# First convolution of a four-layer network: where degrees, residual input, batch scale and activation are computed

## The reference

```python
emb = jnp.einsum('bnc,ec->bne', x_flat, dist_w)                 # 16 numbers per position
d2 = sq[:, :, None] + sq[:, None, :] - 2.0 * jnp.einsum('bne,bme->bnm', emb, emb)
...
adj = knn_mask & (dist <= THRESHOLD)                            # 24 nearest, within 10
adj = adj | jnp.eye(N, dtype=bool)[None]
X_lin = x_flat @ fc_w.T + fc_b
Dv = jnp.clip(jnp.sum(adj_f, axis=2), EPS, None)
De = jnp.clip(jnp.sum(adj_f, axis=1), EPS, None)
S = (adj_f / De[:, None, :]) @ adj_f.transpose(0, 2, 1) / Dv[:, :, None]
out_flat = S @ X_lin + x_flat
...
o = (out - mean) * rsqrt(var + BN_EPS) * bn_gamma + bn_beta     # over the batch, per channel
return o * jax.nn.sigmoid(o)
```

## Time and profile before

| | us |
|---|---|
| median of three runs | 802.1 |
| lowest, highest run | 801.76, 804.69 |
| the profiled execution, its own time | 801.38 |
| its span, first to last instruction | 799.6 |
| PE busy, share of the span | 598.2, 75% |
| DVE | 515.9, 65% |
| ACT | 378.7, 47% |
| POOL | 281.8, 35% |

### The profile page before, as it was taken

The page is one execution under the profiler, slowest core; times in us unless marked ns, Lnnn a source line. Parts: engine busy times, 40 slices in busy tenths (PEclk is TensorE's granted clock), DMA queues, the critical chain, the costliest instruction groups (busy, mean ns, idle before and its releaser), DMA issues. The chain is left out here.

```text
span 799.6 us, 8259 instructions
## 1 busy us (share of the span) xinstructions
PE 598.2 (75%) x2455; PEld 355.4 (44%) x2455; DVE 515.9 (65%) x1237; ACT 378.7 (47%) x565; POOL 281.8 (35%) x211
## 2 busy tenths in 40 slices
PE   4652779999993798482997764799596986988760
PEld 2442557777772583261444431534344334821110
DVE  2794576767764625566935564864296954759966
ACT  2102657887782450253436550472131343769930
POOL 4997167787784100301006650500101760000000
PEclk9999999999996799675996556598587995589985
DMA  3431000000001400402000000200101000000000
GB/s 105 125 98 44 0 2 1 1 1 1 0 2 36 75 0 1 148 1 79 4 1 0 1 1 10 71 1 0 63 0 27 1 1 8 1 0 0 0 0 14
DMA packets 18436, 18.44 MB, mean 23 GB/s; under 512 B 10938, under 2 KB 14331, under 8 KB 18008
## 3 DMA queue, kind: packets, MB, share of 16 engines
q1 hardware_dynamic: 18392, 17.93, 8.6%
HBM read 17.02 MB, written 0.26 MB: 22 GB/s over the span
## 5 line engine op out<-in xcount | busy, mean ns | idle before, releaser
L647 POOL TENSOR_TENSOR l0f_hid_lo<-l0f_hid,l0f_hid_hi 114x512 fp32r<-114x512 f32 (+1 forms) x75 | 97.9, 1314 | 53.3 <-ACT l0f_hid_hi L729 52.4
L825 DVE TENSOR_TENSOR l0f_hid<-l0f_silu,PS 114x512 f32<-114x512 f32 x96 | 65.6, 686 | 41.0 <-ACT l0f_silu L746 39.9
L683 PE MATMUL PS<-l0f_xs,l0w_hi 128*114 128x512 f32 x192 | 78.4, 408 | 0.0
L683 PE MATMUL PS<-l0f_xs,l0w_lo 128*114 128x512 f32 x192 | 77.2, 402 | 0.0
L746 ACT ACTIVATE l0f_silu<-PS 114x512 f32<-114x512 f32 x96 | 57.6, 600 | 31.1 <-PE PS L683 30.3
L2471 PE MATMUL PS<-l3f_ring,l3f_slots 128*32 128x512 f32 x128 | 55.7, 661 | 12.8 <-DVE l3f_ring L2548 12.8
L1303 POOL TENSOR_TENSOR l2c_den<-l2c_far,l2c_den 128x1024 f32<-128x1024 f32 x16 | 37.5, 2356 | 64.8 <-ACT l2c_den L1461 64.8
L729 ACT CAST l0f_hid_hi<-l0f_hid 114x512 fp32r<-114x512 f32 x96 | 59.1, 615 | 2.4 <-DVE l0f_hid L825 1.9
L2548 DVE SCALAR_TENSOR_TENSOR l3f_ring<-l3f_ring,l_countT 128x1024 f32<-128x1024 f32 x32 | 38.9, 1220 | 10.0 <-ACT l3f_ring L2498 10.0
L2494 ACT ACTIVATE l3f_ring<-l3r_plain,l3r_neg 128x1024 f32<-128x1024 f32 x32 | 36.0, 1134 | 14.2 <-PE PS L2471 9.7
L2542 DVE SCALAR_TENSOR_TENSOR l3f_ring<-l3f_slope,l3r_low,l3f_ring 128x1024 f32<-128x1024 f32 x32 | 40.8, 1279 | 0.9 <-ACT l3f_ring L2494 0.9
(11 more groups left out here) (571 smaller groups left out, 1359.6 us busy)
## 6 DMA issues: line engine op xcount, KB each, us to landing
l0w_raw<-in_l_w SPq DMA_DIRECT2D x32, 170.5 KB, 3.2
l3k_edge<-in_edges SPq DMA_DIRECT2D x2, 1024.0 KB
l2c_wqkv<-in_l_wqkv SPq DMA_DIRECT2D x3, 384.0 KB, 4.1
l0w_w<-in_l_w SPq DMA_DIRECT2D x8, 142.5 KB
l2f_raw<-in_l_w SPq DMA_DIRECT2D x2, 512.0 KB, 6.1
l1c_pos_w<-in_l_pos_w SPq DMA_DIRECT2D x1, 784.0 KB, 4.8
l1c_vrow<-l1c_vimg SPq DMA_DIRECT2D x7, 88.0 KB, 3.7
l1f_raw<-in_l_w SPq DMA_DIRECT2D x2, 256.0 KB
```

What stands on the lines that cost most here:

```text
L647: g.tensor_tensor(hid_lo[0:k, q % HIDS, :], hid[0:k, q % HIDS, :], hid_hi[0:k, q % HIDS, :], ALU.subtract).then_inc(S("low_pool"), 1)
L683: last = t.matmul(m.PS[0:k, (one, two)[z], :], half[:, e, z, a:a + k], xs[:, h * HALF:(h + 1) * HALF], start=(half is ew.hi), stop=(half i ...
L825: v.tensor_tensor(hid[0:k, at % HIDS, :], silu[0:k, at % RING0, :], m.PS[0:k, two, :], ALU.mult).then_inc(S("free"), 1)
```

## The change

It does six things in `l0_conv_stage`.

1. The embedding is released by halves: the semaphore `emb` counts each half, and it lies in banks 0 and 1 instead of 2 and 3. PE starts the first two images' distances when the first half's four rows are there.
2. The eight matmuls of the linear layer move behind the distances of the second image.
3. `degrees` is gone; `token_means` takes the degree from column 65 of the token product, and `edge_means(1)` moves ahead of `token_means(0)`.
4. The addition of `Xn` on DVE is gone. In place of each transpose of `mixed` PE does two plain matmuls with the identity as the moving operand, one on `Xn` and one on `mixed`, that add up in PSUM.
5. Scale and shift are made by ACT, with three dependent activations on 64 numbers, after DVE's reciprocal; a small silu ahead of them brings its table in.
6. One silu of the scaled and shifted input, by halves, writes `Y`; `lo`, `sig` and their product are gone.

```diff
         @block.scalar
...
-            a.wait_ge(S("emb"), 1)
             for h in range(2):
                 half = slice(h * HALF, (h + 1) * HALF)
+                a.wait_ge(S("emb"), h + 1)
                 if h == 0:
                     a.wait_ge(S("minus"), 4)
-                a.copy(right[0:EMB, half], m.PS[0:EMB, 2 + h, :]).then_inc(S("rows"), 1)
+                a.copy(right[0:EMB, half], m.PS[0:EMB, h, :]).then_inc(S("rows"), 1)
...
             batch_stats_scalar(a, m, C, agg, "l0c_bn")
-            a.wait_ge(m.sem("l0c_bn_affine"), 1)
+            a.activation(agg[:, 7:8], m.ident[0:C, 0:1], ACT.Silu).then_inc(S("table"), 1)
+            a.wait_ge(S("rdev"), 1)
+            a.activation(aff[:, 0:1], bn[:, 0:1], ACT.Copy, scale=agg[:, 4:5]).then_inc(S("scale"), 1)
+            a.wait_ge(S("scale"), 1)
+            a.activation(agg[:, 5:6], agg[:, 0:1], ACT.Copy, scale=aff[:, 0:1]).then_inc(S("scale"), 1)
+            a.wait_ge(S("scale"), 2)
+            a.activation(aff[:, 1:2], agg[:, 5:6], ACT.Identity, bias=bn[:, 1:2], scale=-1.0).then_inc(S("scale"), 1)
+            a.wait_ge(S("scale"), 3)
             for h in range(2):
                 part = slice(h * HALF, (h + 1) * HALF)
-                a.activation(lo[:, part], m.PS[0:C, h, :], ACT.Identity, bias=aff[:, 1:2], scale=aff[:, 0:1]).then_inc(S("act"), 1)
-                a.activation(sig[:, part], m.PS[0:C, h, :], ACT.Sigmoid, bias=aff[:, 1:2], scale=aff[:, 0:1]).then_inc(S("act"), 1)
+                a.activation(m.Y[:, part], m.PS[0:C, h, :], ACT.Silu, bias=aff[:, 1:2], scale=aff[:, 0:1]).then_inc(S("act") if h == 0 else m.sem("y_ready"), 1)
 
         @block.tensor
...
             for h in range(2):
-                last = t.matmul(m.PS[0:EMB, 2 + h, :], dist_w[:], m.XT[0:C, h * HALF:(h + 1) * HALF], start=True, stop=True)
-            last.then_inc(S("emb"), 1)
-            for j in range(NB):
-                last = t.matmul(m.PS[:, 6, j * C:(j + 1) * C], m.XT[:, j * P:(j + 1) * P], fc_w[:], start=True, stop=True)
-            last.then_inc(S("lin"), 1)
-            t.wait_ge(S("rows"), 8)
+                t.matmul(m.PS[0:EMB, h, :], dist_w[:], m.XT[0:C, h * HALF:(h + 1) * HALF], start=True, stop=True).then_inc(S("emb"), 1)
             for b in range(B):
+                if b % 2 == 0:
+                    t.wait_ge(S("rows"), 2 * b + 4)
...
                 last.then_inc(S("dist"), 1)
+                if b == 1:
+                    for j in range(NB):
+                        last = t.matmul(m.PS[:, 6, j * C:(j + 1) * C], m.XT[:, j * P:(j + 1) * P], fc_w[:], start=True, stop=True)
+                    last.then_inc(S("lin"), 1)
             t.transpose(m.PS[:, 7, 0:P], m.ident[:], m.ident[:]).then_inc(S("eye"), 1)
...
-            for j in range(NB):
-                if j % 4 == 0:
-                    t.wait_ge(S("mixed"), j // 4 + 1)
-                last = t.transpose(m.PS[0:C, j // 4, (j % 4) * P:(j % 4 + 1) * P], mixed[:, j, :], m.ident[:])
+            for h in range(2):
+                t.wait_ge(S("mixed"), h + 1)
+                for j in range(4 * h, 4 * h + 4):
+                    dst = m.PS[0:C, h, (j % 4) * P:(j % 4 + 1) * P]
+                    t.matmul(dst, m.Xn[:, j, :], m.ident[:], start=True, stop=False)
+                    last = t.matmul(dst, mixed[:, j, :], m.ident[:], start=False, stop=True)
             last.then_inc(S("mixed_turned"), 1)
...
         @block.vector
...
             def token_means(h):
 
                 v.wait_ge(S("token"), h + 1)
                 tok_ps = m.PS[:, 6 + h, 0:4 * (C + 1)].rearrange("p (q c) -> p q c", q=4)
-                part = mixed[:, 4 * h:4 * h + 4, :]
-                do(v.tensor_tensor(part, tok_ps[:, :, 0:C], over(deg[:, 1, 4 * h:4 * h + 4], [P, 4, C]), ALU.mult))
-                v.tensor_tensor(part, part, m.Xn[:, 4 * h:4 * h + 4, :], ALU.add).then_inc(S("mixed"), 1)
+                share = deg[:, 1, 4 * h:4 * h + 4]
+                do(v.tensor_scalar(share.unsqueeze(2), tok_ps[:, :, C:C + 1], 1e-9, None, ALU.max))
+                do(v.reciprocal(share, share))
+                v.tensor_tensor(mixed[:, 4 * h:4 * h + 4, :], tok_ps[:, :, 0:C], over(share, [P, 4, C]), ALU.mult).then_inc(S("mixed"), 1)
...
-            degrees(0)
-            degrees(1)
+            edge_means(1)
             token_means(0)
-            edge_means(1)
             token_means(1)
```

More of the change, by code:

```diff
@@ L336, in l0_conv_stage @@
         stats, agg, aff = sb("stats", [C, 2, 6]), sb("agg", [C, 8]), sb("aff", [C, 2])
-        sig, lo = sb("sig", [C, T]), sb("lo", [C, T])
         S = lambda name: m.sem("l0c_" + name)
@@ L365, in _ @@
             norm_scalar(a, m)
-            a.wait_ge(S("emb"), 1)
             for h in range(2):
                 half = slice(h * HALF, (h + 1) * HALF)
+                a.wait_ge(S("emb"), h + 1)
                 if h == 0:
                     a.wait_ge(S("minus"), 4)
-                a.copy(right[0:EMB, half], m.PS[0:EMB, 2 + h, :]).then_inc(S("rows"), 1)
-                a.mul(left[0:EMB, half], m.PS[0:EMB, 2 + h, :], 2.0).then_inc(S("rows"), 1)
-                a.activation(left[32:32 + EMB, half], m.PS[0:EMB, 2 + h, :], ACT.Square).then_inc(S("rows"), 1)
-                a.activation(right[64:64 + EMB, half], m.PS[0:EMB, 2 + h, :], ACT.Square).then_inc(S("rows"), 1)
+                a.copy(right[0:EMB, half], m.PS[0:EMB, h, :]).then_inc(S("rows"), 1)
+                a.mul(left[0:EMB, half], m.PS[0:EMB, h, :], 2.0).then_inc(S("rows"), 1)
+                a.activation(left[32:32 + EMB, half], m.PS[0:EMB, h, :], ACT.Square).then_inc(S("rows"), 1)
+                a.activation(right[64:64 + EMB, half], m.PS[0:EMB, h, :], ACT.Square).then_inc(S("rows"), 1)
             a.wait_ge(S("lin"), 1)
@@ L487, in edge_means @@
                 v.tensor_tensor(edge[:, 4 * h:4 * h + 4, 0:C], edge_ps[:, :, 0:C], over(share, [P, 4, C]), ALU.mult).then_inc(S("edge_sb"), 1)
-            def degrees(h):
-                share = deg[:, 1, 4 * h:4 * h + 4]
-                v.wait_ge(S("inc"), 2 * h + 2)
-                do(v.tensor_reduce(share, work[:, 4 * h:4 * h + 4, :], AX.X, ALU.add))
-                do(v.tensor_scalar(share, share, 1e-9, None, ALU.max))
-                do(v.reciprocal(share, share))
             def token_means(h):
@@ L521, in _ @@
             v.wait_ge(S("w"), 48)
-            batch_stats_vector(v, m, C, [m.PS[0:C, 0, :], m.PS[0:C, 1, :]], stats, agg, 1e-5,
-                               bn[:, 0:1], bn[:, 1:2], aff[:, 0:1], aff[:, 1:2], "l0c_bn")
-            v.wait_ge(S("act"), 4)
-            v.tensor_tensor(m.Y[:], lo[:], sig[:], ALU.mult).then_inc(m.sem("y_ready"), 1)
+            for j in range(2):
+                do(v.bn_stats(stats[:, j, :], m.PS[0:C, j, :]))
+            do(v.bn_aggr(agg[:, 0:2], stats[:]))
+            v.tensor_scalar(agg[:, 2:3], agg[:, 1:2], 1e-5, None, ALU.add).then_inc(m.sem("l0c_bn_var"), 1)
+            v.wait_ge(m.sem("l0c_bn_dev"), 1)
+            v.reciprocal(agg[:, 4:5], agg[:, 3:4]).then_inc(S("rdev"), 1)
             back_vector(v, m)
```

## The result

The changed kernel takes 795.65 us (median of five runs, 793.55 to 796.05), the kernel before, on the same chip, 802.1 (801.72 to 804.69). The ratio is 0.991, with a 95% interval of 0.9889 to 0.993. The forecast was 795.7, and the mechanism behind it was that GpSimd's weight work ends the stage. The profiled execution took 795.65 us where that of before took 801.38, so 5.7 less; the stage itself is 5.90 shorter, as the next one starts at 76.15 instead of 82.05.

The account below looks back on a forecast made before the run. The handover chain of DVE, PE and ACT bounded the stage, with GpSimd's split ending last once it shrinks. The next stage starts 6.0 us sooner: 801.38 - 6.0 = 795.4, said as 795.7 for the median, range 793.5 to 798.8.

Parts of the forecast that it names:

- Part 1: Embedding by halves, linear layer later: DVE starts at 20.0 but waits for `eye`; taken as 0, ends -1.3 and +0.8 us.
- The wait for GpSimd: DVE's threshold operations at later images: whether DVE or GpSimd goes first is worth up to 0.84 us to DVE.
- Part 2: Degrees from the column of ones: DVE's 6.2 us leave the chain; second token products start at 56.68 instead of 60.82.
- Part 3: Input added by PE in the mixing: sixteen plain fp32 matmuls at 0.43, 6.83 us plus 0.2 tail, nearly cancelling earlier savings.
- the bound of 4.2 from below: Low end for the mixing's sixteen plain matmuls, in us, each at a transpose's 1.06/4; the high end was 7.4.
- Rival C: A plain matmul costs four transpose spacings, 0.85, so mixing takes 13.6 us; 801.7, no change; chance 0.04.
- Part 4: Affine on ACT and one silu, behind the statistics: 5.9 us; PE starts its transposes 5.8 us after the statistics.
- rival B: ACT's tail is longer, three dependent operations at 2.3 us: 796.5, or 797.8 with a second table load; chance 0.10.
- The end: Stage's end: chain would release at 75.5, but GpSimd ends at 75.54; next stage at 76.0 instead of 82.05, 6.0 us gained.
- D: Rival: the stage gains, but part is lost again behind it in waits between engines and loads: 798.5; chance 0.05.
- E: Rival: slower through the PE clock in the next stage; 10 us at 1.2 GHz give 805.4; chance 0.03.
- The sum: Whole kernel: 801.38 - 6.0 = 795.4; a median may lie higher than the profiled run, so 795.7.

Follow-up runs that it names:

- The last experiments: Turned identity put directly behind image 0's distances, in the changed kernel without ACT affine and single silu (796.93 us) and in the relieved, fused kernel with strided threshold (789.13 us).
- the kernel with part 4 alone: The kernel before with only scale and shift by ACT and one silu by halves added: 797.08 us, ratio 0.9929.
- the one with `eye` early: The changed kernel with ACT affine and single silu undone, and the turned identity directly behind image 0's distances: 796.93 us, ratio 0.9946.
- the pair with GpSimd relieved: Changed kernel with upper `l0w_w2p` parts made by ACT and strided threshold: `Xn` added by PE's plain matmuls 795.31 us, by DVE's fused multiply-add 791.44 us.
- the two with GpSimd relieved: The changed kernel with upper `l0w_w2p` parts made by ACT instead of GpSimd: 795.82 us; the same with a strided threshold: 795.31 us.
- the kernel with part 3 undone: The changed kernel with `mixed` transposed on PE and `Xn` added on DVE again: 795.91 us, ratio 0.9926.

## Why the prediction was right, step by step

- **Part 1.** DVE at 20.14 (20.0 was forecast), the idle time before the incidence 3.61 (3.8). "I take 0" was 0.72 too low: the last edge products start at 53.23 instead of 53.95. At the first threshold DVE lost what the diagonal had gained, as forecast, and 0.21 more, as the GpSimd operation in its way began 0.22 later than before; at the second, third and fourth it went ahead of GpSimd. The last experiments show the reason given, `eye`, to be the true one for the idle time, and another to be as strong: with `eye` early the idle time is gone in both kernels, and once all of it went into GpSimd's operations.
- **The wait for GpSimd.** The step "a few tenths decide whether DVE or GpSimd goes first, which is worth up to 0.84 us" had the mechanism and a size far too small. It was read from one row, 1.27, in which DVE met the end of a short operation. Where it meets the start of a long one the price is 2.2 to 2.9 us each time (2.73 for 0.43 at 30.16 in the kernel with part 4 alone, 3.32 in the one with `eye` early), and hundredths of a microsecond decide. The earlier trace rows had it in L219, 2.91 for 0.15.
- **Part 2.** From the edge means to PE's start 0.88 (55.08 to 55.96), as forecast to the hundredth; then 3.61 to the mixing (3.63). The edge means themselves start 0.72 sooner than the 55.80 of the forecast, which is part 1's error.
- **Part 3.** Sixteen matmuls were to take 7.03 us and took 5.42 (59.57 to 64.99). The price of one was right as long as PE kept its pace, 0.43, and the bound of 4.2 from below was not for nothing: from about 63 on it was 0.22. Rival C's price, 0.85, is refuted by the same rows, and with it the rule of the Trainium skill ("TensorE: Matmul & The Clock Gate", Terms) that the transpose mode is four times faster for fp32: at the slower pace it is 0.213 from one transpose to the next and 0.43 from one plain matmul to the next, a factor of two, and the measurement decides. That part 3 eats much of what part 2 brings is measured too: 2.81 us in the pair with GpSimd relieved, where the fused form stands against it.
- **Part 4.** From the statistics to the transposes back 5.95 us (5.8). The three dependent operations took 0.28 and 0.29, and stand 0.32 apart, instead of 0.24; rival B's bound of 2.3 for the three was far off (0.93).
- **The end.** GpSimd at 75.84 (75.54 was forecast; its first operation starts at 15.59, 0.25 later than before), 0.31 to the next stage (0.49). These two errors are 0.30 late and 0.18 early, so that 76.15 lies closer to the 76.0 of the forecast than its steps do. The chain was to release at 75.5, half a microsecond before GpSimd, and would have done so at 73.3. In that step the forecast was right with more room than it claimed, and the errors in parts 1 and 3, 2.3 us together, could not reach the time for that reason.
- **Behind the stage.** 5.90 in the stage and 5.7 in the span: 0.2 is lost behind it, so D and E did not come. That is no more than such runs vary: in the thirteen profiled executions the time less the start of the next stage is 717.4 to 720.5 us, and the median of a variant gained from 0.3 us less to 1.8 more than its profiled stage did (2.6 more with part 4 alone, where the slowest run was profiled). Where this spread comes from stays open.
- **The sum.** 801.38 less 6.0 is 795.4, and the 0.3 on top follows from nothing: the prediction's own reason, a median as far above the profiled run as before, would have given 796.1. The profiled run is the median here, 795.65. That 795.7 was hit to 0.05 us is luck; what was right is the 6 us and what sets them.

## What to carry to other kernels

A change that shortens a chain is worth the distance to the engine that ends next, and it is cheap to test both sides of that: four useless operations on the chain (no change) and four on the other engine (all of it is seen) settle in two runs what the rows suggest. Move the work of the engine that ends last before polishing the chain, and then price the chain's parts again, since what cost nothing under cover (part 3, here 2.8 us) now counts. Where DVE and GpSimd work at once, give DVE forms that read one operand from PSUM where they can, and don't take a gain of a microsecond for granted when it shifts DVE against GpSimd.

## What the runs showed of the hardware

**DVE and GpSimd.** Thresholds (one input and the output in SBUF, fp32) and operations with two SBUF inputs wait for a GpSimd operation that began before them, however short they are: 2.38 us for 64 numbers. Only behind the last 0.1 us or so of its recorded time did they not (0.43 at 44.56 in the changed kernel, with GpSimd's row ending at 44.67). A `tensor_scalar` of one number per partition didn't wait either: 0.15 at 66.71, with GpSimd at work from 66.52, while one of four numbers did (1.61 in L494). The Trainium skill, page "SBUF — State Buffer", section "SBUF: two separate sides", says that the two share a pair of ports under an exclusive lock, held for the whole instruction by whichever starts first, for DVE in a two-port mode, or with two SBUF inputs against a GpSimd operation that reads SBUF, as the split does. The rows agree: 0.01 us of lead decided 2.30 us, and the fused operation, with one input in PSUM, took 0.86 for four in all its four places. A stride of two didn't take the threshold out of it, and it wasn't slower for the stride (0.43).

**PE's pace in plain fp32 matmuls.** A plain matmul of 128 columns took 0.43 at one pace and 0.22, half of it, at the other, which I read as the two levels of the clock, 1.2 and 2.4 GHz. In this chain the step fell inside the mixing in all seven traces with part 3: at about 63 in the changed kernel, 65.9 and 67.4 in the two with GpSimd relieved, after 3.4, 3.7 and 5.1 us of it, and in the other four at 62.1 to 63.2, after 2.6 to 3.9 us, with PE busy without a pause since the token products before. The 7.19 us of distances show no such step. The granted clock doesn't show the rise: it reads 1.00 at both paces. It does show a fall to 0.50 close to 70 us, after PE had stood idle from 65. All seven traces with part 3 have such a fall between 69 and 73 us, and none of the six without. That fits a rise at 63, and a column that stands at 1.00 up to the first change that was recorded. The windows of the changed kernel (length, busy per engine, granted clock, DMA share, GB/s):

```profile
60.00:62.00 2.00, 2.00 (x12) 2.00 (x11) 0.47 (x2) 0.00 (x0) 2.00 (x2) 1.00 0.71 207
62.00:64.00 2.00, 2.00 (x15) 2.00 (x14) 0.00 (x0) 0.00 (x0) 1.92 (x2) 1.00 0.69 185
...
70.00:75.00 5.00, 1.11 (x8) 0.93 (x8) 0.69 (x1) 0.92 (x2) 4.84 (x4) 0.50 0.00 0
```

The last of these stretches in the kernel with part 3 undone:

```profile
70.00:75.00 5.00, 0.00 (x0) 0.00 (x0) 0.51 (x1) 0.00 (x0) 4.92 (x3) 1.00 0.00 0
```

So a granted clock averaged over the execution can't be compared between these kernels: it is 0.817 with part 3 and 0.833 without (the kernel before). What decides when the step comes was not tried.
